# A wait for each tile's eight indirect transfers, and cosine attention in two token halves beside the first dispatch

## Time and profile before

| | us |
|---|---|
| median of 3 runs | 3179.95 (3172.23 to 3184.66) |
| the profiled execution, its own time | 3171.14 |
| its span | 3169.2 |
| PE busy | 1646.5 (52%) |
| DVE busy | 1357.1 (43%) |
| ACT busy | 956.7 (30%) |
| POOL busy | 1065.9 (34%) |
| POOL, scatter L2029, 512 transfers | 501.7 |
| POOL, gather L2040, 512 transfers | 489.6 |

### The profile page before, as it was taken

How to read it: one execution, slowest core, us unless ns; L and a number is a source line. 1 busy time by engine, 2 the same in 40 slices (tenths; PEclk the granted TensorE clock), 3 DMA queues, 4 the chain that set the end, 5 groups by cost and what they waited for, 6 DMA issues and landing times.

```text
span 3169.2 us, 40618 instructions
## 1 busy us (share of the span) xinstructions
PE 1646.5 (52%) x14020; PEld 1135.9 (36%) x14020; DVE 1357.1 (43%) x3644; ACT 956.7 (30%) x1757; POOL 1065.9 (34%) x1177
## 2 busy tenths in 40 slices
PE   4763113229466624231432494665322456988985
PEld 2542112227344423131321273454211443454454
DVE  3558224213133435641541231335442466676655
ACT  3640000015222331021100151223257733344344
POOL 1003753640354354555337404553570020000001
PEclk8985555559777855565555696777655776898998
DMA  8991111339577611111023495775110000000000
GB/s 241 275 346 35 52 38 50 128 120 384 198 243 225 208 37 31 53 40 36 28 77 103 143 385 185 238 231 195 37 48 7 1 1 1 1 2 1 2 2 27
DMA packets 276793, 352.97 MB, mean 111 GB/s; under 512 B 68624, under 2 KB 161104, under 8 KB 276432
## 3 DMA queue, kind: packets, MB, share of 16 engines
q10 hardware_dynamic: 83984, 153.13, 13.7%
q1 hardware_dynamic: 159840, 130.08, 13.6%
q0 software_dynamic: 32768, 67.17, 6.9%
HBM read 201.35 MB, written 167.51 MB: 116 GB/s over the span
## 4 chain that ended last, share of the span: by engine, by line
PE 31%; another core or an unknown queue 21%; DVE 16%; issue 14%; ACT 12%; DMA 3%; SPq 1%; POOL 1%; ACTq 0%; DVEq 0%; POOLq 0%
ACT arena L1144 6%; PE psum L2260 5%; PE psum L2250 4%; PE psum L2211 4%; PE psum L448 3%; DMA arena<-expert_blocks 3%; PE psum L1595 2%; PE psum L1576 2%; PE psum L432 1%; PE psum L427 1%; ACT arena L1446 1%; DVE X L2010 1%; PE psum L1592 1%; PE psum L1593 1%
## 5 line engine op out<-in xcount | busy, mean ns | idle before, releaser
L2040 POOL DMA_INDIRECT arena<-slot_results,SLOTS x512 | 489.6, 956 | 721.2 <-DMA slot_results<-arena 326.0
L2029 POOL DMA_INDIRECT slot_rows<-arena,SLOTS x512 | 501.7, 980 | 497.7 <-issue 497.7
L1994 DVE COPY arena<-psum 128x512 f32<-128x512 f32 x288 | 196.5, 690 | 811.6 <-remote 492.1
L2083 ACT ACTIVATE arena<-psum 128x512 f32<-128x512 f32 x288 | 172.0, 597 | 646.9 <-PE psum L2211 266.9
L2260 PE MATMUL psum<-arena 64*128 64x128 f32 x2304 | 244.0, 339 | 231.2 <-issue 141.9
L2250 PE MATMUL psum<-arena 128*64 128x128 f32 x2304 | 221.0, 320 | 255.5 <-issue 247.0
L2260 PEld LDWEIGHTS psum<-arena 64*128 64x128 f32 x2304 | 182.3, 222 | 292.7 <-issue 207.6
L2250 PEld LDWEIGHTS psum<-arena 128*64 128x64 f32 x2304 | 142.7, 156 | 318.6 <-issue 304.6
L2211 PE MATMUL psum<-ident,arena 128*128 128x128 f32 x1152 | 223.8, 326 | 17.1 <-DMA arena<-slot_rows 15.8
L169 POOL TENSOR_SCALAR rstd<-mv 128x4 f32<-128x4 f32 x32 | 6.8, 213 | 663.6 <-DVE mv L581 663.3
L2090 ACT ACTIVATE arena<-psum 128x256 f32<-128x256 f32 x288 | 110.4, 383 | 282.3 <-remote 223.8
(11 more groups left out here) (253 smaller groups left out, 3091.6 us busy)
## 6 DMA issues: line engine op xcount, KB each, us to landing
arena<-slot_rows ACTq DMA_DIRECT2D x288, 256.0 KB
slot_results<-arena ACTq DMA_DIRECT2D x288, 256.0 KB
arena<-expert_blocks SPq DMA_DIRECT2D x512, 96.0 KB
slot_rows<-zeros SPq DMA_DIRECT2D x2, 18432.0 KB, 80.4
arena<-own_blocks SPq DMA_DIRECT2D x44, 256.0 KB
slot_rows<-arena,SLOTS POOLq DMA_INDIRECT x512
arena<-slot_results,SLOTS POOLq DMA_INDIRECT x512
expert_blocks<-in_expert_w SPq DMA_DIRECT2D x1, 7680.0 KB, 26.2
```

The source lines that it names most:

```text
L1994: dve.tensor_copy(YSB[:, p].rearrange("p (c h) d -> p h c d", h=2), psum[:, first:first + 2, 0:256].rearrange("p h (c d) -> p h c d", c=2) ...
L2029: pool.indirect_dma_start(out=slot_rows[h], out_offset=bass.IndirectOffsetOnAxis(ap=slots_of(t, k), axis=0), in_=XNH[:, t], in_offset=None ...
L2040: pool.indirect_dma_start(out=GATHERED[:, n % TPI, k], out_offset=None, in_=slot_results[h], in_offset=bass.IndirectOffsetOnAxis(ap=slots_ ...
L2083: act.activation(XSBT[:, g % 2], psum[:, g % 2, :], ACT.Copy).then_inc(c_xt.sem, 1)
```

## The change

`dispatch` and `gather` wait, before a tile's eight indirect transfers, until the eight of the tile before have landed (not before a half's first tile):

```diff
@@ def dispatch(pool, run, h)
                 pool.wait_ge(s_idx.sem, s_idx.at(run, t // TPI))
+                if t % HTILES:
+                    pool.wait_ge(d_rows[h][(t - 1) % TPI].sem, d_rows[h][(t - 1) % TPI].at(run, (t - 1) % HTILES // TPI))
                 stand(pool)
@@ def gather(pool, run, h)
                 pool.wait_ge(g_sum.sem, g_sum.at(run, n - TPI))
+                if n % HTILES:
+                    pool.wait_ge(g_rows[(n - 1) % TPI].sem, g_rows[(n - 1) % TPI].at(run, (n - 1) // TPI))
                 stand(pool)
```

Attention takes a first and a last step, and is called for steps 0 to 3 ahead of the first half's routing and for steps 4 to 7 ahead of the second half's. The barrier after it goes; the wait for the remaining weights moves to the engines' lists:

```diff
@@ def middle_vector(dve)
-            own_tiles(dve)
             for h in range(HALVES):
+                cos_vector(dve, 0, HSTEPS * h, HSTEPS * h + HSTEPS)
+                if h == 0:
+                    own_tiles(dve)
+                dve.wait_ge(loaded_all, 16 * (len(weights) - FIRST_WEIGHTS))
                 route_half(dve, 0, h, nothing)
@@ def middle_scalar(act)
             for h in range(HALVES):
+                cos_scalar(act, 0, HSTEPS * h, HSTEPS * h + HSTEPS)
                 route_scalar(act, 0, h)
+            act.wait_ge(loaded_all, 16 * (len(weights) - FIRST_WEIGHTS))
@@ def middle_tensor(pe)
             for h in range(HALVES):
+                cos_tensor(pe, 0, HSTEPS * h, HSTEPS * h + HSTEPS)
+                pe.wait_ge(loaded_all, 16 * (len(weights) - FIRST_WEIGHTS))
                 route_tensor(pe, 0, h, nothing)
```

POOL has no part in attention's steps any more. The deviations go to ACT (a square root) and DVE (an inversion), the padded values to DVE; the hardware loops are written out:

```diff
@@ def cos_vector(dve, layer, begin, end)
+            def stats_of(s):
                 front_stats(dve, s, layer)
+
+            def scale(s):
+                invert(dve, s, layer)
                 front_scale(dve, s, layer)
+            def padded(s):
+                dve.wait_ge(a_qkv.sem, a_qkv.at(0, s))
+                dve.wait_ge(a_av.sem, a_av.before(0, s - 1))
+                for n in range(4):
+                    dve.tensor_copy(VP[:, s % 2, :, n:8:4, DH * n:DH * n + DH],
+                                    QKV[:, :, 128:192].rearrange("p t (h d) -> p t h d", d=DH)[:, :, n:8:4, :]).then_inc(a_vp.sem, 1)
+            def step(i):
+                left = end - 1 - i
                 if left >= 1:
                     normal(i + 1)
+                if left >= 2:
+                    scale(i + 2)
+                if i > begin:
                     add(i - 1)
...
+                if left >= 2:
+                    padded(i + 2)
@@ def cos_scalar(act, layer, begin, end)
+            def spread(s):
+                deviations(act, s, layer, first_eps[:, 0:1], EPS)
```

SP fills the first half's `slot_rows` ahead of the copies of the expert weights and the second half's behind them; each half has its own semaphore, and POOL waits for it ahead of each dispatch:

```diff
@@ def middle_gpsimd(pool)
-            pool.wait_ge(cleared, 16 * HALVES)
             for run in range(2):
                 for h in range(HALVES):
+                    pool.wait_ge(cleared[h], 16)
                     dispatch(pool, run, h)
@@ block.sync
+            sp.wait_ge(constants, CONSTANTS)
+            clear(0)
             sp.dma_start(block_of[:, 0:INTER], whole[:, 0:INTER]).then_inc(blocked, 16)
...
+            own_parts(STAYS.rearrange("p n (m c) -> p (n m) c", c=2 * D), slice(0, STAYING * GROUP // 2), blocked)
+            clear(1)
+            sp.wait_ge(blocked, 16 * 11)
```

More of the change, by code:

```diff
@@ L284, in step @@
                 divide(i)
[L286 to L301, removed]
+                if left >= 2:
+                    padded(i + 2)
+            dve.wait_ge(constants, CONSTANTS + 3)
+            stats_of(begin)
+            scale(begin)
+            stats_of(begin + 1)
+            squares(begin)
+            padded(begin)
+            normal(begin)
+            scale(begin + 1)
+            stats_of(begin + 2)
+            keys(begin, begin % 2)
+            squares(begin + 1)
+            padded(begin + 1)
+            for i in range(begin, end):
+                step(i)
+            add(end - 1)
+            dve.wait_ge(a_x.sem, a_x.at(0, end - 1))
         def psum_b16(bank):
@@ L453, in weigh_values, with cos_tensor @@
             return mm
-        def cos_tensor(pe, layer):
-            pe.wait_ge(constants, 17)
+        def cos_tensor(pe, layer, begin, end):
+            pe.wait_ge(constants, CONSTANTS + 3)
             def project(s):
@@ L508, in output, with step @@
                 mm.then_inc(a_y.sem, 1)
-            def step(i, u, first=False, left=STEPS):
+            def step(i):
+                u, left = i % 2, end - 1 - i
                 scores(i, u, 0)
                 scores(i, u, 1)
-                if not first:
+                if i > begin:
                     output(i - 1)
@@ L529, in step @@
                 values(i, u, 3)
[L531 to L546, removed]
+            front_tensor(pe, begin, layer)
+            project(begin)
+            pe.wait_ge(a_qkv.sem, a_qkv.at(0, begin))
+            transposes(begin)
+            front_tensor(pe, begin + 1, layer)
+            pe.wait_ge(a_qt.sem, a_qt.at(0, begin))
+            pe.wait_ge(a_kt.sem, a_kt.at(0, begin))
+            project(begin + 1)
+            for i in range(begin, end):
+                step(i)
+            output(end - 1)
         def earlier(layer):
@@ L1773, in program @@
         GATHERED = view([P, TPI, TOPK, D])
-        cleared = semaphore("cleared")
+        cleared = [semaphore(f"cleared{h}") for h in range(HALVES)]
         blocked = semaphore("blocked")
-        stays = semaphore("stays")
         e_stat = signal("e_stat", HTILES, HALVES)
```

120 lines of the change are left out of this document (46 added, 74 removed).

## The result

Three interleaved rounds on one chip gave 2829.3 us median (2821.7 to 2832.2, four runs) against 3177.2 for the kernel before on that chip: ratio 0.890, interval 0.8874 to 0.8925. The profiled span is 2827.4 us. The sign was right, the size was not.

The account below looks back on a forecast made before the run. PE's signals, held during POOL's unbroken indirect transfers, were taken to bound the kernel. Terms -28 - 60 - 65 - 30 - 10 - 41 + 20 = -214 took 3171.1 to 2957, plus 9 for the median: 2966 us, range 2860 to 3120.

Parts of the forecast that it names:

- What bounds the kernel: Whole kernel: PE's signals to ACT and DVE lag with the length of POOL's unbroken runs of indirect transfers.
- The wait per tile: POOL between eights: next eight begins 2.9 us after the last issue, lag clears at 2.6; a tile takes 11.73 us.
- The slower rival: Tile borders: waits don't clear the lag, eights add up like one long run; +173, 3353 us, chance 0.10.
- Second dispatch with the experts: Second dispatch and its second-run counterpart: eights let expert groups pass at 3.98 us each; gains 60 and 65 us.
- Gather beside the experts: Gather's first 57 us: its first four tiles become eights, 14 groups instead of 10; gain 15 us per run.
- Attention in two halves: Start to second dispatch: first dispatch at 208, second half's attention beside it slowed 1.6 times, second dispatch at 480; gain 28.
- Gather beside GLRU: 1085 to 1335 us: ten borders cost 16 us, DVE's order sets the pace, signals pass sooner; -10 us.
- Third dispatch and GLRU's second half: From 1335 us: GLRU's last four steps at 33.5 us each instead of 44, longer dispatch hidden; -41 us.
- Last gather: 2195 to 2385 us: eleven back-to-back borders cost 1.6 to 2.5 us each; +20 us.
- After it: Last gather's last issue to the end: no term in the sum, 785 us predicted against 785.2 before.
- free passage: Rival for the whole kernel: signals pass nearly freely, groups at 3.0 us; -361, 2819 us, chance 0.13.
- The rival that DVE keeps POOL from its descriptors: First dispatch: all 128 transfers at 2.12 us add 149 us; total 3031 us, chance 0.05.

Follow-up runs that it names:

- the wait alone: Kernel before plus POOL's two waits per tile, attention in one piece: 2803.8 against 3172.6 us on chip 14 (0.884), 1.144 on chips where the kernel before takes 2427.
- the halves alone: Changed kernel without its waits per tile, against the kernel before: 3197.3 against 3172.6 us on chip 14 (1.007), 0.982 on chips 8 and 15.
- quiet_waits: Changed kernel with waits only in the first half's dispatches and second half's gathers: 2986.8 us against 3180.8 for the kernel before on chip 0 (0.938).
- the pause: Changed kernel with three memsets to an unused tile replacing each wait: 2807.2 us against 3172.6 for the kernel before on chip 14 (0.884), 1.034 on chip 15.

## Why the prediction was wrong in size

By its own steps:

*What bounds the kernel.* Confirmed. On late chips PE's signals are held while POOL issues; on prompt chips no trace shows such a wait, and the kernel before is 750 us faster. That the lag depends on the chip was not foreseen.

*The wait per tile.* Right in mechanism, and by a narrow margin. The slower rival hung on whether the next eight starts before signals clear, at 2.6 us: 3.1 us was measured, 2.87 suffices, 1.66 does not (where between the last two it turns was not tried). An undisturbed tile of a dispatch took 11.95 us instead of 11.73, 0.2 more per border.

*Second dispatch with the experts* (-60, -65): -57.6 and -63. The price of a group taken from the gather stage, 3.98 us, came out as 3.96. *Gather beside the experts* (-15 each): -15 and -15, with the 14 groups in its first 57 us.

*Attention in two halves* (-28): -22.6, but for another reason than given. With the wait alone the second dispatch starts at 484.7, with both at 484.9 (chips 14 and 3; without the last gather's waits, which come later, it was 472.6 on chip 14). The halves bring the first dispatch forward by 84 us, to 202.8, and the second half's attention, whose additions come 25 to 36 us apart beside it, gives back nearly all of them. The gain there belongs to the waits. Where no wait breaks the run, the half stands still until the dispatch ends, as the bound (loss 62) had it in kind: with the halves alone its first addition starts at 405.2, 38 us after the last issue, and the second dispatch at 527.0, 19 later than before.

*Gather beside GLRU* (-10): -49.5. *Third dispatch and GLRU's second half* (-41): -72. *Last gather* (+20): +4.5. *After it* (0): -51.6. These four are the failed step. Their excess is 39, 31, 15 and 52 us, 137; less the 10 by which the other terms fell short this is 127 of the 128 us between the forecast span (2955) and the measured one.

The first GLRU term took it that DVE's order sets the pace beside the gather, and so freed almost nothing there; yet the fourth addition itself had waited 15.22 us for an unknown sender. The second term was priced with 33.5 us a step, from these same first four steps. They ran beside gathers in eights to 24s, so they still held the lag that the change removes. Additions after the change:

```profile
1025.05 0.69 DVE L682 TENSOR_TENSOR X<-psum,X 128x512 f32<-128x512 f32 x1 [5.67 <-PE psum L796]
...
1078.36 0.69 DVE L682 TENSOR_TENSOR X<-psum,X 128x512 f32<-128x512 f32 x1 [5.74 <-PE psum L796]
...
1274.90 0.69 DVE L682 TENSOR_TENSOR X<-psum,X 128x512 f32<-128x512 f32 x1 [5.47 <-issue]
```

Four steps end 83.8 us after the second gather's first issue (994.6), the last four 84.1 us after the third dispatch's (1190.8): 21 us a step. GLRU then sets no pace at all. `quiet_waits`, which has its waits in just these two stages and two others like them, takes 196.8 and 197.7 us for the two as well. From 994.6 to 1595.4 POOL issues 384 transfers in 48 tiles without a longer break, 12.5 us a tile, and POOL's own end, which the prediction had as the bound of the third dispatch (-75), is what came out (-72).

The last gather was priced by its borders alone. The layer beside it was held by the same lag; freed, it does 136 of its scan's activations earlier. That term was set to 0 by leaving it out.

The chance of 0.13 for free passage was too small for a related reason: groups and attention did not pass freely (3.96 us a group against 2.5 on a prompt chip), yet the sum of that rival came within 10 us. That was luck: it gave 71 us too much to the groups, 57 to the attention and 10 to the gathers, and 61 too little to GLRU (-60 against -121) and 57 to the last gather.

The rival that DVE keeps POOL from its descriptors is refuted: POOL's first dispatch took 199.4 us from first to last issue, and the longest of the 512 dispatch transfers after the change is 2.1 us, as before.

```profile
L2027 POOL DMA_INDIRECT slot_rows<-arena,SLOTS x512: 955/961/2131, 202.8 to 1595.4; - x171
```

By the factor of the Trainium skill ("SBUF — State Buffer", "SBUF: two separate sides"), put on every transfer, it would have been an estimated 600 us; this trace does not agree with that. Single transfers are longer beside DVE, though not beside the copies that the change gave it (16 of 0.2 us; the transfers that they fell into took 0.96). The longest one:

```profile
207.30 1.49 DVE L1962 TENSOR_TENSOR_SCAN arena<-ones_row,arena 128x640 f32<-128x640 f32 x1
207.43 2.13 POOL L2027 DMA_INDIRECT slot_rows<-arena,SLOTS  x1 [0.30 <-issue]
```

The four longest all start 0.13 or 0.14 us into this scan of 1.49 us and end 0.77 us after it, and so does the 2.12 us of the kernel before. The nine that start 1.0 us into the scan take 1.27 us and end at the same distance behind it. So the longest transfer was not one beside copies, as the prediction took it.

## What to carry to other kernels

When an engine's long runs of indirect transfers hold other engines' signals, count what every neighbour does beside them, and price each freed stage by a row taken where the cause is absent, not by its mildest case. A stop in the issue pays only if it is longer than the time that the run before it needs to clear. That condition fits all runs here and is not proven. Wait for nothing in it that can itself be late, and time the kernel on several chips: this change is 11 to 12% faster on some and 11% slower on others, while the halves alone are 1.8% faster on those others.

## What the runs showed of the hardware

- The same program takes 2427 us on chips 8 and 15 and 3171 to 3181 us on chips 0, 3 and 14. On the slow ones signals of PE to ACT and DVE are held while GpSimd issues indirect transfers every 1.27 us. No trace from chips 8 and 15 has such a wait. What differs is not known, nor whether it is the chip: each was timed on one occasion.
- Held signals pass 2.6 us after the last of 8 transfers, 3.6 to 4.4 us after 15 or 16, 6.1 us after 128. A gap of 2.87 us after each 8 had the whole gain of the waits; one of 1.66 us after each 8, or 3.1 us after each 16, did not.
- The four longest of the 512 dispatch transfers (2.12 to 2.13 us on POOL, where the median is 0.96) each start 0.13 or 0.14 us after a 1.49 us scan of DVE has started and end 0.77 us after it; nine more that start 1.0 us into it take 1.27 us and end as far behind it.
- The eight transfers of a tile land 2.1 us after their last issue in quiet, and up to some 6 us after it beside 273 GB/s. The Trainium skill ("DMA: Bandwidth & Descriptors", "Anatomy of one DMA — SWDGE (gpsimd) path") puts the fixed part of such a transfer at about 2.0 us, constant; the quiet value agrees, the loaded one, which takes in whatever queueing there was, is three times it.
- No version is the best on both kinds of chip. On late chips the whole change (0.881 and 0.890), the wait alone and the pause (0.884 each) are within 1% of each other; on prompt ones the pause costs 3.4%, the whole change 11.2%. Untried are a stop between 1.66 and 2.87 us, and one of over 4.4 us after each 16.
